# A four-layer graph network: the second layer's edge sum split between strips of a weighted matrix and gathers, with a small clear between all gathers

## The chip, the cores and the metric

The kernel runs on 1 core of one Trainium2 chip. The metric is the device time of one execution in microseconds (us), lower is better. Before the change the median of 3 runs is 6407.87 us (6407.16 to 6411.51).

## The reference, cut to what matters

A graph has 6250 nodes with 128 features and 100000 edges sorted by target; each layer's result is added to x and normalised. The four layers differ in how they sum over edges:

```python
edge_index = jnp.stack([src, dst])
x = _layernorm(x + _L0_gnn_ref(...))   # mean of h[dst] over src, twice; no weights
x = _layernorm(x + _L1_gnn_ref(...))   # the second layer:
    # msg = edge_weight[:, None] * x[src]
    # agg = segment_sum(msg, dst); h = relu((x + agg) @ W1 + b1); return h @ W2 + b2
x = _layernorm(x + _L2_gnn_ref(...))   # four propagation steps: segment_sum(x[src], dst) / degree, and attention
x = _layernorm(x + _L3_gnn_ref(...))   # h1 = relu([x[src], x[dst], edge_attr] @ W1.T + b1); sum over dst; a GRU cell
```

The targets are drawn as 6250 u^2, so the first edges crowd on few nodes: a tile of 128 sorted edges spans few targets at the start and many at the end.

## The kernel before, in words

The edges are cut into 784 tiles of 128; four tiles are a group, 196 groups. Everything is written out engine by engine, each engine works in its program order, and semaphores tie them; no planner decides anything. A stage ends with a barrier of all engines.

`prepare_edges` loads and transposes the edge lists and builds tables (indices, targets relative to a group's first target, unit offsets) with many short VectorE instructions on one partition. `build_adjacency` builds a dense 6272 x 6272 matrix of edge counts in bf16 in memory, strip by strip: for each tile it compares an iota with a key per edge (`hot`, line 656), multiplies it with a one-hot of the low source bits (line 725), and ScalarE copies the sums into a slab.

`dense_pass` multiplies that matrix with node rows split into three bf16 terms (21 matmuls for each of its blocks of 7 x 128 rows and 512 columns, line 1145). It is used twice in the first layer (all of the matrix, 91 blocks) and in each of the four steps of the third layer, where only a part of the matrix is multiplied and the remaining tiles are gathered beside it (line 1069): 244 tiles in steps 1 and 4, 344 tiles in steps 2 and 3.

`layer1_pass` is the second layer's edge sum, all by gathers. For each group POOL issues four indirect DMAs (line 1415, 128 rows of 512 bytes each), ScalarE scales the rows by the edge weights (line 1432), VectorE makes one-hots (line 1456), TensorE multiplies rows by one-hots, and a matrix of ones by one-hots for the degrees (lines 1492, 1493), and VectorE adds both results to the accumulator (line 1451). `layer1_nodes` then writes the degrees out and applies the layer's two matrices.

`message_pass` is the fourth layer's edge stage: 784 gathers (line 2139), and for each group edge features are loaded, transposed and multiplied, added to the gathered rows (`meet`, line 2206), rectified and summed.

Each of these passes is followed by a second version for graphs whose targets spread too widely, which is branched over here.

Of the kernel before, what the change touches and what calls it, by code (L numbers as in the profile page):

```python
# [59 lines left out]
AC = N + max(COLUMNS) + 6  # L60
FILLED = 320
# [30 lines left out]
def gnn_resnorm(nc, out, x, src, dst, edge_attr_128, edge_weight,  # L92
# [6 lines left out]
    with ctx:  # L99
# [84 lines left out]
        tail_loc = sb("tail_loc", [P, TAILS])  # L184
        tail_base = sb("tail_base", [1, TAILS // K + GU], I32)
# [15 lines left out]
        rdeg_row, deg_row, dinv_row = dram("rdeg_row", [NP]), dram("deg_row", [NP]), dram("dinv_row", [NP])  # L201
        loc_rows = dram("loc_rows", [TILES, P], I16)
# [117 lines left out]
        def prepare_edges():  # L320

            with ExitStack() as st:
# [16 lines left out]
                offs, bad = tmp("offs", [1, UP]), tmp("bad", [1, 6, UP])  # L339
# [3 lines left out]
                of_tile = tmp("of_tile", [1, 2, TILES])  # L343
                units = len(UNITS)
                with stage("cleared", "e_in", "dve_done", "turned", "copied", "info_out", "rows_out", "group_in", "info_in", "based",
                           "row_done", "spread", "col_done", "tabs_out") as (
                        block, cleared, e_in, dve_done, turned, copied, info_out, rows_out, group_in, info_in, based,
                        row_done, spread, col_done, tabs_out):
# [7 lines left out]
                    def _(sp):  # L356
# [24 lines left out]
                        sp.dma_start(dst_index, dst_idx[:, :]).then_inc(tabs_out, 16)  # L381
                        sp.wait_ge(rows_out, 32)
                        sp.wait_ge(tabs_out, 64)

                    @block.vector
                    def _(dve):
# [76 lines left out]
                        for heads, split in SPLITS.items():  # L463
# [16 lines left out]
                        after(40)  # L480
# [3 lines left out]
                        after(43)  # L484
                        nc.vector.tensor_scalar(offs[:, :], offs[:, :], 0.0, None, ALU.max).then_inc(row_done, 1)
                        nc.vector.tensor_reduce(worst[:, 0:1], worst[:, :], AX.X, ALU.max).then_inc(row_done, 1)
                        after(45)
# [16 lines left out]
                        nc.vector.tensor_tensor(two(again[:, :]), two(dst_c[:, :]), ps[:, 4:6, 0:TILES // 2], ALU.is_equal).then_inc(col_done, 1)  # L504
                        done(8)
                        for c in CLASSES:
# [26 lines left out]
                    def _(pe):  # L533
# [9 lines left out]
                        for n in range(2):  # L543
# [3 lines left out]
                            lastmm.then_inc(spread, 1)  # L547

# [392 lines left out]
        def dense_pass(n, table, heads, transposed=False, split=None, phases=()):  # L941
# [7 lines left out]
            with ExitStack() as st:  # L949
# [4 lines left out]
                adj = tmp("adj", [P, RING, GW, BLOCK], BF16)  # L954
                if groups:
                    rows = tmp("rows", [P, GR * K, heads * P])
                    onehot = tmp("onehot", [P, OH, K, P])
# [6 lines left out]
                with stage(*names) as (block, *s):  # L964
# [156 lines left out]
                    def _(pe):  # L1121
                        for t in range(tiles + 1):
# [11 lines left out]
                            if t == tiles:  # L1134
                                break
# [1348 lines left out]
```

## Time and profile before

| | us |
|---|---|
| median of 3 runs | 6407.87 |
| the profiled execution | 6403.48 |
| its span | 6401.9 |
| PE, DVE, ACT, POOL busy | 4821.9, 2547.6, 1447.4, 2736.0 |
| granted TensorE clock, mean | 0.882 |

Where the span goes, by the first and last instructions of the stages: the edge tables 0 to 112 us, the adjacency matrix to about 1000, the first layer to about 1970, the second layer's edge sum to 2967, the third layer from there to about 5240, the message pass from 5248 to about 6236, and the rest. Times below are microseconds from the start of the span. A row of the timeline gives the start, the length, the engine, the line, the tiles, how many instructions were merged, and in brackets how long the engine had been idle and who released it. fp32 matmuls stand in the records as two.

### The profile page before, as it was taken

To read this page: it belongs to the slowest core of one execution; us is meant where nothing else is said; L and a number is where in the kernel's file an instruction comes from. 1 tells how busy PE (TensorE), PEld (TensorE's weight loads), DVE (VectorE), ACT (ScalarE), POOL (GpSimd) and SP (SyncE) were. 2 spreads that over 40 slices of the span, in tenths; PEclk is the share of its full clock that TensorE was granted. 3 is DMA by queue.
4 is the path that set the end of the run, shared out by engine and by line. 5 is a ranking of instruction groups with operands and counts; after the bars stand their busy time and mean duration, and the time that the engine had idled before them with its cause. 6 is when DMAs were issued, how large, how long until landed. Compare 5 with 4: busy or idle time off the path is not lost. (4 is left out here: it accounts for less than half of the span.)

```text
span 6401.9 us, 87750 instructions
## 1 busy us (share of the span) xinstructions
PE 4821.9 (75%) x28467; PEld 3336.5 (52%) x28706; DVE 2547.6 (40%) x6483; ACT 1447.4 (23%) x2559; POOL 2736.0 (43%) x2767
## 2 busy tenths in 40 slices
PE   1677665997995556555798799989978967777675
PEld 0444333444444555554654376657656556676663
DVE  5678773001004222224546633252242354444445
ACT  0467772001002222222101100010010022222222
POOL 2000000000004777773355177557717727777770
PEclk6789887998997777777799899999999989989987
DMA  1166998997982222221565688688868755555541
GB/s 59 45 87 119 134 149 171 204 202 170 202 177 65 52 52 52 52 52 47 159 197 169 217 264 257 214 275 253 250 211 259 238 146 144 144 141 145 142 119 41
DMA packets 1485756, 973.04 MB, mean 152 GB/s; under 512 B 698166, under 2 KB 1407150, under 8 KB 1485424
## 3 DMA queue, kind: packets, MB, share of 16 engines
q1 hardware_dynamic: 1147613, 599.81, 38.3%
q0 software_dynamic: 99376, 228.31, 13.2%
q10 hardware_dynamic: 238500, 141.37, 7.7%
q8 instruction: 167, 2.74, 0.2%
q14 instruction: 100, 0.82, 0.0%
HBM read 652.10 MB, written 162.95 MB: 127 GB/s over the span
## 5 line engine op out<-in xcount | busy, mean ns | idle before, releaser
L1145 PE MATMUL ps<-adj_d,xs_d 128*128 128x512 bf16 (+1 forms) x7699 | 1704.8, 379 | 162.3 <-DVE xs_d L1114 149.2
L1145 PEld LDWEIGHTS ps<-adj_d,xs_d 128*128 128x128 bf16 x7938 | 782.5, 100 | 1023.4 <-DVE xs_d L1114 153.0
L1415 POOL DMA_INDIRECT rows_g<-x_tab,idx_g x784 | 743.0, 948 | 1246.0 <-ACT idx_g L1424 1007.4
L1069 POOL DMA_INDIRECT rows_d<-xh_tab,src_idx x688 | 697.6, 1014 | 446.9 <-POOLq L158 222.6
L2139 POOL DMA_INDIRECT rows_m<-p_tab,idx_m x784 | 750.9, 958 | 282.1 <-issue 237.8
L725 PE MATMUL ps<-hot,lo 128*128 128x500 bf16 (+4 forms) x2052 | 536.7, 385 | 299.7 <-DVE hot L656 153.2
L1492 PE MATMUL ps<-onehot_g,rows_g 128*128 128x128 f32 x1568 | 422.8, 363 | 426.1 <-ACT rows_g L1432 303.2
L1069 POOL DMA_INDIRECT rows_d<-x_tab,src_idx x488 | 489.5, 1003 | 537.7 <-POOLq L158 285.0
L767 ACT CAST slab<-ps 128x1000 f32 (+4 forms) x530 | 558.1, 1053 | 366.3 <-PE ps L743 167.2
L1492 PEld LDWEIGHTS ps<-onehot_g,rows_g 128*128 128x128 f32 x1568 | 333.5, 263 | 462.7 <-issue 303.8
L2266 PE MATMUL ps<-win_m,turned_hot_m 128*128 128x128 f32 x1568 | 330.5, 294 | 195.9 <-DVE pre_m L2206 195.1
L656 DVE TENSOR_SCALAR hot<-iota_key,key_col 128x1225 bf16<-128x1225 int16 (+4 forms) x782 | 414.9, 562 | 115.3 <-PE ps L743 73.7
L1131 PEld LDWEIGHTS ps<-onehot_d,rows_d 128*128 128x128 f32 x3728 | 443.2, 192 | 32.9 <-issue 16.9
L1131 PE MATMUL ps<-onehot_d,rows_d 128*128 128x128 f32 x3728 | 452.8, 276 | 2.0 <-DMA rows_d<-xh_tab,src_idx 2.0
L1432 ACT ACTIVATE rows_g<-rows_g,ew_col 128x128 f32<-128x128 f32 x784 | 271.8, 394 | 698.3 <-DMA rows_g<-x_tab,idx_g 698.3
L1044 ACT COPY acc<-ps 128x512 f32<-128x512 f32 (+1 forms) x54 | 31.0, 574 | 1706.2 <-PE ps L1145 1491.8
L1493 PE MATMUL ps<-onehot_g,ones_mat 128*128 128x128 f32 x1568 | 403.6, 350 | 0.0
L725 PEld LDWEIGHTS ps<-hot,lo 128*128 128x128 bf16 x2052 | 159.7, 103 | 444.2 <-ACT slab L767 204.8
L2266 PEld LDWEIGHTS ps<-win_m,turned_hot_m 128*128 128x128 f32 x1568 | 252.8, 203 | 225.1 <-issue 220.4
L1451 DVE TENSOR_TENSOR acc<-acc,ps 128x256 f32 x196 | 82.7, 422 | 676.9 <-PE ps L1493 676.9
L605 POOL MEMSET slab<- 128x6528 bf16 x1 | 5.5, 5537 | 808.3 <-DMA adjacency<-slab 808.3
L1493 PEld LDWEIGHTS ps<-onehot_g,ones_mat 128*128 128x128 f32 x1568 | 337.1, 265 | 0.0
(322 smaller groups left out, 6115.7 us busy)
## 6 DMA issues: line engine op xcount, KB each, us to landing
adj_d<-adjacency SPq DMA_DIRECT2D x196, 896.0 KB
attr_m<-in_edge_attr SPq DMA_DIRECT2D x195, 256.0 KB
k_rows_d<-k_tab ACTq DMA_DIRECT2D x56, 448.0 KB, 4.3
loc_m<-loc_rows SPq DMA_DIRECT2D x196, 128.0 KB
adjacency<-slab SPq DMA_DIRECT2D x4, 4900.0 KB
q_s<-q_tab SPq DMA_DIRECT2D x42, 448.0 KB
rden_s<-rden_tab SPq DMA_DIRECT2D x42, 448.0 KB
xh_tab<-rows_s ACTq DMA_DIRECT2D x42, 448.0 KB
```

The lines of the kernel that those rows point to most:

```text
L656: nc.vector.tensor_scalar(hot[:, t % HOT, 0:w], iota_key[:, 0:w], key_col[:, t:t + 1], None, ALU.is_equal).then_inc(hot_made, 1)
L725: last = nc.tensor.matmul(ps[:, bank(k, b), 0:to], lo1[:, slot, n, :], hot[:, t % HOT, b * w:b * w + to], start=(t == u.tile), stop=(k == ...
L767: nc.scalar.copy(slab(c)[:, 0:banks * u.per_bank, bass.ds(at[k % 8], u.width)].rearrange("p (b h) r -> p b h r", b=banks), ps[:, s:s + ban ...
L1069: nc.gpsimd.indirect_dma_start(rows[:, q % GR * K + k, :], None, table, bass.IndirectOffsetOnAxis(ap=src_idx[:, j:j + 1], axis=0)).then_in ...
L1131: last = nc.tensor.matmul(sums_of(q)[:, h, :], rows[:, q % GR * K + k, h * P:(h + 1) * P], onehot[:, q % OH, k, :], start=(k == 0), stop=( ...
L1145: last = nc.tensor.matmul(ps[:, m % 2, 0:w], xs[:, g * GW + k, e, :], adj[:, slot, k, 0:w], start=(g == 0 and k == 0 and e == 0), stop=(g ...
L1415: nc.gpsimd.indirect_dma_start(rows[:, j, :], None, x_tab, bass.IndirectOffsetOnAxis(ap=idx[:, q, k:k + 1], axis=0)).then_inc(rows_in[j // ...
L1432: last = nc.scalar.activation(rows[:, j, :], rows[:, j, :], ACT.Copy, scale=ew_col[:, bass.ds(i * U + j, 1)])
L1492: nc.tensor.matmul(sums_of(q)[:, 0, :], rows[:, j, :], hot, start=(k == 0), stop=(k == K - 1))
L1493: last = nc.tensor.matmul(sums_of(q)[:, 1, :], ones_mat[:, :], hot, start=(k == 0), stop=(k == K - 1))
L2139: nc.gpsimd.indirect_dma_start(rows[:, q, k, :], None, p_tab, bass.IndirectOffsetOnAxis(ap=idx[:, q, k:k + 1], axis=0)).then_inc(rows_in[2 ...
L2266: nc.tensor.matmul(ps[:, 2 + q % 2, c], turned_hot[:, q % 2, c], win[:, q % R, :], start=True, stop=False)
```

## The change

There are four parts.

1. `layer1_pass` is written anew. The first 292 tiles are no longer gathered. For each of them VectorE makes a one-hot of the source's low 7 bits (`lo1`, 128 columns) and one of a key made of the source's high bits and the target's place in a narrow window (`hot`, 343 or 490 columns); ScalarE multiplies `lo1` by three bf16 terms of the edge weight (`lo_w`); TensorE multiplies the three with `hot` into a strip; VectorE adds the strip into a `slab` of 49 x 144 columns in fp32. 98 tiles work in pairs of two to a unit, with 7 target columns (343 wide); 42 in pairs and 152 alone, with 10 (490 wide): 222 units. The units fall into 8 chunks. Behind each chunk a sweep reads all of x in 7 windows of 448 KB and multiplies them with the slab (49 fp32 matmuls of 144 columns), and ScalarE clears the slab. The other 492 tiles, 123 groups, are gathered as before, one group due about every 2.4 strip tiles. The matmuls with ones are gone; the accumulator holds one part instead of two.
2. The degrees now come from the first dense pass (`count=True`): VectorE sums each block of the matrix along its columns, and the sums are turned and written out at that stage's end.
3. `prepare_edges` makes the keys, the low bits and the strips' offsets, and writes them to memory.
4. In all three kinds of gathering passes POOL clears a 128 x 64 fp32 tile `pause` behind every gather (492 + 1176 + 784 = 2452 in all), and waits for the clear before the last one.

The branched-over version of the second layer's pass is now `general_pass` with weights.

```diff
@@ dense_pass (POOL)
                                     nc.gpsimd.indirect_dma_start(
                                         rows[:, q % GR * K + k, :], None, table,
                                         bass.IndirectOffsetOnAxis(ap=src_idx[:, j:j + 1], axis=0)).then_inc(rows_in[q % GR], 16)
+                                    if j > tail:
+                                        pool.wait_ge(paced, j - tail)
+                                    nc.gpsimd.memset(pause[:, :], 0.0).then_inc(paced, 1)
@@ dense_pass (VectorE, with count)
+                            if count and t < tiles:
+                                w = place(m // blocks, m % blocks)[2]
+                                dve.wait_ge(adj_in[t % RING], 16 * (t // RING + 1))
+                                nc.vector.tensor_reduce(parts[:, g * GW:(g + 1) * GW, m:m + 1], adj[:, t % RING, :, 0:w], AX.X, ALU.add).then_inc(tallied, 1)
@@ message_pass (POOL)
+                                    pool.wait_ge(paced, n * U + q * K + k + 1)
+                                    nc.gpsimd.sem_inc(begun, 1)
+                                    nc.gpsimd.memset(pause[:, :], 0.0).then_inc(paced, 1)
@@ layer1_pass (new)
+            GR, OH, AHEAD, BANKS, HOTS, XS = 10, 6, 4, 2, 3, 2
+                    for q in range(groups):
+                        due[q * WT // groups].append(q)
...
+                    @block.gpsimd
+                        for q in range(groups):
+                            if q >= GR:
+                                pool.wait_ge(group_done, q - GR + 1)
+                            for k in range(K):
+                                j = (first_group + q) * K + k
+                                nc.gpsimd.indirect_dma_start(
+                                    rows[:, q % GR, k, :], None, x_tab,
+                                    bass.IndirectOffsetOnAxis(ap=src_idx[:, j:j + 1], axis=0)).then_inc(rows_in[q % GR], 16)
+                                if q or k:
+                                    pool.wait_ge(paced, q * K + k)
+                                nc.gpsimd.memset(pause[:, :], 0.0).then_inc(paced, 1)
...
+                    @block.scalar
+                        def blanken(c):
+                            if c:
+                                act.wait_ge(x_used, c * G)
+                            nc.scalar.copy(slab[:, :, :], zero[:, 0:1].unsqueeze(2).to_broadcast([P, WIN, WC])).then_inc(blank, 1)
...
+                        def weigh(t):
+                            act.wait_ge(lo_made, t + 1)
+                            if t >= HOTS:
+                                act.wait_ge(stripped, WUNIT_OF[t - HOTS] + 1)
+                            for e in range(TERMS):
+                                last = nc.scalar.activation(lo_w[:, t % HOTS, e, :], lo1[:, t % HOTS, :], ACT.Copy, scale=weight[:, e, t:t + 1])
+                            last.then_inc(lo_weighted, 1)
...
+                        for t in range(WT):
+                            weigh(t)
+                            for q in due[t]:
+                                scale(q)
+                            if t in sweep_at:
+                                blanken(sweep_at[t] + 1)
...
+                    @block.vector
+                        for t in range(WT):
+                            pick(t)
+                            u = WUNIT_OF[t]
+                            if t == WUNITS[u].tile and u >= 2:
+                                enter(u - 2)
+                            for q in due[t]:
+                                match(q + AHEAD)
+                                add(q)
...
+                    @block.tensor
+                        for t in range(WT):
...
+                            for e in range(TERMS):
+                                last = nc.tensor.matmul(strip(u), lo_w[:, t % HOTS, e, :], hot[:, t % HOTS, 0:w],
...
+                            for q in due[t]:
+                                sum_group(q)
+                            if t in sweep_at:
+                                sweep(sweep_at[t])
```

`add(q)` waits for `group_done` of group q; `sum_group(q)` waits for the scaled rows, the one-hots and the add two groups back; `pick` makes `lo1` and `hot`; `enter` adds a strip to the slab.

On POOL, at the head of the message pass, before (the four gathers of a group follow one another):

```order
240 L2139 DMA rows_m<-p_tab,idx_m 128x128 x4
241 L2136 REGISTER_ALU
242 L2139 DMA rows_m<-p_tab,idx_m 128x128 x4
243 L2136 REGISTER_ALU
244 L2139 DMA rows_m<-p_tab,idx_m 128x128 x4
```

and now:

```order
3551 L2356 DMA rows_m<-p_tab,idx_m 128x128
3552 L2359 ISA
3553 L2361 MEMSET pause 128x64
3554 L2356 DMA rows_m<-p_tab,idx_m 128x128
3555 L2359 REGISTER_ALU
3556 L2361 MEMSET pause 128x64
```

Between any two gathers there now stands a clear, and a semaphore step ahead of it.

On DVE in the second layer's pass, before (L1456 makes a group's one-hots; the add, L1451, comes behind the one-hots of the groups ahead):

```order
1463 L1456 TENSOR_SCALAR onehot_g<-iota,loc_col 128x128
1464 L1456 ISA
1465 L1456 TENSOR_SCALAR onehot_g<-iota,loc_col 128x128
1466 L1456 ISA
1467 L1456 TENSOR_SCALAR onehot_g<-iota,loc_col 128x128
1468 L1456 ISA
1469 L1456 TENSOR_SCALAR onehot_g<-iota,loc_col 128x128
```

and now, in the later part where each tile is a unit of its own (L1644 and L1645 are `pick`, L1657 `enter`, L1616 `match`, L1631 `add`):

```order
2081 L1657 TENSOR_TENSOR slab_g<-slab_g,ps 128x49x10
2082 L1616 TENSOR_SCALAR onehot_g<-iota,loc_col 128x128 x4
2083 L1631 ISA
2084 L1631 TENSOR_TENSOR acc<-acc,ps 128x128
2085 L1644 TENSOR_SCALAR lo_g<-iota,lo_g 128x128
2086 L1645 TENSOR_SCALAR hot_g<-iota_key_g,key_g 128x490
2087 L1644 TENSOR_SCALAR lo_g<-iota,lo_g 128x128
2088 L1645 TENSOR_SCALAR hot_g<-iota_key_g,key_g 128x490
```

The one-hot `lo1` of the next strip tile stands behind the add of the group before it.

On PE in the same pass, before (rows and ones in turn):

```order
3022 L1492 MATMUL ps<-onehot_g,rows_g 128x128
3023 L1493 MATMUL ps<-onehot_g,ones_mat 128x128
3024 L1492 MATMUL ps<-onehot_g,rows_g 128x128
3025 L1493 MATMUL ps<-onehot_g,ones_mat 128x128
3026 L1492 MATMUL ps<-onehot_g,rows_g 128x128
```

and now, around the first sweep (L1707 are strips, L1683 a gathered group, L1694 the sweep):

```order
3105 L1707 MATMUL ps<-hot_g,lo_w_g 128x490 x6
3106 L1683 MATMUL ps<-onehot_g,rows_g 128x128 x4
3107 L1707 MATMUL ps<-hot_g,lo_w_g 128x490 x6
3108 L1694 MATMUL ps<-slab_g,xp_g 128x144 x49
3109 L1707 MATMUL ps<-hot_g,lo_w_g 128x490 x3
3110 L1683 MATMUL ps<-onehot_g,rows_g 128x128 x4
```

Strips, groups and sweeps share one in-order queue.

## Rows read from the trace of the kernel before

**Rows 1.** The page, part 5: the message pass's gathers (busy, mean ns, idle before):
```profile
L2139 POOL DMA_INDIRECT rows_m<-p_tab,idx_m x784 | 750.9, 958 | 282.1 <-issue 237.8
```

**Rows 2.** Busy times in stretches (length; PE, PEld, DVE, ACT, POOL; clock; DMA):
```profile
1120.00:1280.00 160.00, 159.21 (x728) 72.50 (x741) 0.00 (x0) 2.93 (x5) 0.00 (x0) 1.00 0.95 204
2500.00:2600.00 100.00, 57.92 (x320) 54.05 (x320) 25.59 (x104) 29.11 (x100) 75.62 (x81) 0.78 0.21 52
3800.00:3850.00 50.00, 49.74 (x325) 35.38 (x329) 12.63 (x53) 0.59 (x1) 36.78 (x39) 1.00 0.82 249
5600.00:5650.00 50.00, 39.02 (x288) 37.13 (x288) 22.51 (x75) 12.84 (x32) 37.81 (x41) 0.87 0.54 143
```

**Rows 3.** Timeline of the second layer's edge sum, its gathers, and its start:
```profile
1976.11 0.48 ACT L1424 COPY idx_g<-src_idx 128x4 int32<-128x4 int32 x4 [0.77 <-PEq L158]
...
2299.07 0.94 POOL L1415 DMA_INDIRECT rows_g<-x_tab,idx_g  x1 [0.30 <-issue]
2300.32 0.94 POOL L1415 DMA_INDIRECT rows_g<-x_tab,idx_g  x1 [0.30 <-ACT idx_g L1435]
```

**Rows 4.** The adds of that pass, line L1451 (min/median/max ns, first and last start):
```profile
L1451 DVE TENSOR_TENSOR acc<-acc,ps x196: 420/422/424, 1996.0 to 2966.9; 128x256 f32 x196
```

**Rows 5.** Who waited for whom (total us, times, longest): 3640 to 4180, then 5300 to 6200:
```profile
POOL rows_d L1069 <- issue: 102.1, 335, 0.3
POOL rows_d L1069 <- PE ps L1131: 9.7, 8, 2.1
...
DVE pre_m L2206 <- DMA rows_m<-p_tab,idx_m: 379.8, 134, 5.0
```

**Rows 6.** Timeline of the second layer's edge sum, one group at two TensorE clocks:
```profile
2302.41 0.63 PE L1493 MATMUL ps<-onehot_g,ones_mat 128*128 128x128 f32 x2
2302.83 0.64 PE L1492 MATMUL ps<-onehot_g,rows_g 128*128 128x128 f32 x2
...
2309.80 0.39 ACT L1432 ACTIVATE rows_g<-rows_g,ew_col 128x128 f32<-128x128 f32 x1
2310.33 0.46 PE L1492 MATMUL ps<-onehot_g,rows_g 128*128 128x128 f32 x2 [2.72 <-ACT rows_g L1432]
2311.84 0.69 ACT L1432 ACTIVATE rows_g<-rows_g,ew_col 128x128 f32<-128x128 f32 x2 [1.57 <-DMA rows_g<-x_tab,idx_g]
2311.97 0.39 PE L1493 MATMUL ps<-onehot_g,ones_mat 128*128 128x128 f32 x2
2312.58 0.42 DVE L1451 TENSOR_TENSOR acc<-acc,ps 128x256 f32 x1 [3.54 <-PE ps L1493]
2312.92 1.03 DVE L1456 TENSOR_SCALAR onehot_g<-iota,loc_col 128x128 f32<-128x128 int16 x4
```

**Rows 7.** Timelines elsewhere: short and wide instructions of DVE and ACT:
```profile
74.86 0.28 DVE L413 COPY ends<-infos 1x278 f32<-1x278 f32 x1
175.49 0.61 DVE L656 TENSOR_SCALAR hot<-iota_key,key_col 128x490 bf16<-128x490 int16 x2 [0.79 <-PE ps L736]
1978.93 10.72 DVE L1444 MEMSET acc<- 128x12800 f32 x1 [7.94 <-issue]
3050.75 0.94 ACT L1617 COPY xg_k<-xT 128x896 f32 x1 [6.23 <-PE ps L1596]
3054.71 2.02 DVE L1639 TENSOR_REDUCE knorm_k<-kk_k 128x14 f32<-128x1792 f32 x1
```

**Rows 8.** The page, part 6: one 448 KB load, us to landing:
```profile
k_rows_d<-k_tab ACTq DMA_DIRECT2D x56, 448.0 KB, 4.3
```

**Rows 9.** POOL's timeline: memsets after one another, and a gather after a wait:
```profile
0.91 0.20 POOL L280 MEMSET ident<- 128x128 f32 x1 [0.29 <-POOLq L2474]
1.06 0.20 POOL L281 MEMSET ones_mat<- 128x128 f32 x1
...
3210.16 2.03 PE L1131 MATMUL ps<-onehot_d,rows_d 128*128 128x128 f32 x16
3211.57 0.94 POOL L1069 DMA_INDIRECT rows_d<-x_tab,src_idx  x1 [1.86 <-PE ps L1131]
```

More of the change, by code:

```diff
@@ L60 @@
 AC = N + max(COLUMNS) + 6
+WT, WPAIRS, WNARROW = 292, 70, 49
+WUnit = namedtuple("WUnit", "tile tiles width")
+WUNITS = [WUnit(2 * k, 2, 7 if k < WNARROW else 10) for k in range(WPAIRS)]
+WUNITS += [WUnit(t, 1, 10) for t in range(2 * WPAIRS, WT)]
+WUNIT_OF = [k for k, u in enumerate(WUNITS) for n in range(u.tiles)]
+WFIRSTS = (0, 49, 74, 102, 128, 152, 176, 199)
+WENDS = WFIRSTS[1:] + (len(WUNITS),)
+WC = 144
+WKEYS = WIN * 10
+WROW = 224
 FILLED = 320
@@ L966, in dense_pass @@
                     at = RING + SPLIT + GR
-                    high, left, middle, low, used, stored, cleared, matched, group_done, added = s[at:at + 10]
-                    at += 10
+                    high, left, middle, low, used, stored, cleared, matched, group_done, added, tallied, deg_turned, deg_copied, deg_out, paced = s[at:at + 15]
+                    at += 15
                     for work in works:
@@ new lines, in layer1_pass @@
+                part, left = tmp("part", [P, WT], BF16), tmp("left", [P, WT])
+                at = tmp("at", [1, WROW + len(WFIRSTS)], I32)
+                zero = tmp("zero", [P, 1])
+                names = [f"rows_in{q}" for q in range(GR)] + [f"x_in{k}" for k in range(XS)]
+                names += ["tabs_in", "listed", "cleared", "terms", "matched", "scaled", "group_done", "added", "hot_made", "lo_made",
+                          "lo_weighted", "stripped", "entered", "blank", "x_used", "paced"]
@@ L1480, in _ @@
+                        for u in range(len(WUNITS) - 2, len(WUNITS)):
+                            enter(u)
+                        place(len(WFIRSTS) - 1, len(after_group) + len(after_place))
                     @block.tensor
                     def _(pe):
[L1482 to L1494 removed]
@@ L1496, in _, with sum_group @@
-                        rounds(nc.tensor, f"wide_g{tag}_pe", wide_path, steps, step)
+                        def sum_group(q):
+                            pe.wait_ge(matched, q + 1)
+                            if q >= BANKS:
+                                pe.wait_ge(added, after_group[q - BANKS])
+                            pe.wait_ge(scaled, q + 1)
+                            for k in range(K):
+                                last = nc.tensor.matmul(sums_of(q), rows[:, q % GR, k, :], onehot[:, q % OH, k, :], start=(k == 0), stop=(k == K - 1))
+                            last.then_inc(group_done, 1)
@@ new lines, in sweep @@
+                        def sweep(c):
+                            pe.wait_ge(entered, WENDS[c])
+                            if c:
+                                pe.wait_ge(added, after_place[c - 1])
+                            for g in range(G):
+                                n = c * G + g
+                                pe.wait_ge(x_in[n % XS], 16 * (n // XS + 1))
+                                for k in range(GW):
+                                    last = nc.tensor.matmul(ps[:, 6, 0:WC], xp[:, n % XS, k, :], slab[:, g * GW + k, :],
+                                                            start=(g == 0 and k == 0), stop=(g == G - 1 and k == GW - 1))
+                                last.then_inc(x_used, 1)
```

334 lines of the change are left out of this document (229 added, 105 removed).

## The prediction

> **What bounds the kernel now.** I read the page first, then busy times by stretch, then the timelines inside the two stages whose POOL rows look alike, then the waits. In the second layer's edge sum POOL issues a gather every 1.25 us (start to start in [rows 3]; 81 in 100 us in [rows 2]). Each takes 0.94 us and is followed by 0.30 us in which POOL waits for nothing that the profile shows, while PE is busy 58 us of 100, DVE 26, ACT 29 [rows 2]. So POOL sets the pace: 784 x 1.25 = 980 us, and the pass runs from 1976.1 [rows 3] to the add at 2966.9 and its 0.42 us [rows 4], 991 us. The message pass is the same picture: 784 gathers of 0.958 us, mean, with 238 us of bare issue between them [rows 1], and `meet` waits 380 us for gathered rows [rows 5]. Its pitch is 50 us / 40.2 = 1.245 us (busy 37.81 of 50 in [rows 2], with gap 0.30). In the third layer's steps 2 and 3 two engines are at their limit: PE is busy 49.74 of 50 us at full clock [rows 2], and POOL, with 335 of some 344 gathers behind a bare 0.3 us in step 2, waits for PE 9.7 us in all [rows 5]. In the first layer's dense passes PE is busy 159.21 of 160 us [rows 2].
>
> **The second layer's pass.** POOL falls from 784 to 492 gathers: 492 x 1.25 = 615 us if the pitch stays. That would save 365 us, if the other engines kept up, and by busy time they seem to: ACT has 3 x 292 + 492 = 1368 activations at 0.30 us (a pair ends in 0.69, one in 0.39 [rows 6]) and 8 slab clears, some 450 us; DVE comes to about 460 (292 x 0.52 for `lo1` and `hot`, 492 x 0.26, 222 x 0.65, 123 x 0.29, by the durations below). But the order of the instructions ties them into one chain. At a tile on which a group is due, DVE makes `lo1`; ACT weighs it three times, then scales four gathered tiles; PE can only then do the group; DVE waits for the group to add it, and only behind this add stands the next tile's `lo1`. The chain, from rows:
> - DVE `lo1` until ACT can start: 0.35 us (a compare of 128 columns lasts 0.30 where four take 1.03 [rows 6]).
> - ACT: seven activations, six pitches of 0.30, and 0.53 from the last one's start to PE's (2309.80 to 2310.33 [rows 6]): 2.33.
> - PE: an fp32 matmul of 128 x 128 takes 0.23 at the high clock (2310.33 to 2311.97 is seven of them) and 0.42 at the low (2302.41 to 2302.83) [rows 6]. I take 0.30, since the granted clock was 0.78 [rows 2] and PE will again be half idle: four are 1.20.
> - PE to DVE: the last of the eight matmuls starts at 2311.97 and takes 0.23, the add starts at 2312.58 [rows 6]: 0.39. The add, half as wide as that one of 0.42, 0.29.
> Sum 4.56 us for each of 123 such tiles, 561 us. The other 169 tiles are paced by DVE: `lo1` 0.25, `hot` 0.27 (two of 490 columns in 0.61, [rows 7], where one lasts 0.34), `enter` of 490 fp32 columns at about 1.1 us per 1000 (896-column rate of the sum of 1792 in 2.02 [rows 7]) with its start, 0.7: 1.22 us, 206 us.
> A sweep is 49 fp32 matmuls of 144 columns, 49 x 0.30 x 144/128 = 16.5 us, but needs seven loads of 448 KB with two in flight; one lands in 4.3 us [rows 8], so I take 20. Behind it ACT clears 7056 columns before it may weigh: at 0.94 us for 896 less a start of 0.3 [rows 7] some 5.3 us. PE stands still for that. Seven sweeps at 25.3 and the last at 20: 197 us. The start is the clear of `acc` (half of 10.72 [rows 7]) and the first slab clear, 11 us.
> Together 561 + 206 + 197 + 11 = 975 us against 991: 16 us less. Almost all of POOL's gain is lost, and POOL has 360 us to spare at its present pitch. Bounds: with the high clock throughout and loads hidden, 123 x 0.28 + 8 x 4 less, 910; with the low clock throughout, 123 x 0.48 and 8 x 3 more (49 x 0.42 x 144/128 is 23 us a sweep), 1058.
>
> **The edge tables.** Some 36 short instructions on one partition at about 0.28 us (278 columns [rows 7]), a few wider, and three more stores ahead of the barrier: 11 us more (6 to 16).
>
> **The degrees.** 3584 bf16 columns for each block at 1.13 ns (2.02 us for 1792 [rows 7]) are 4.0 us on DVE, idle there [rows 2]; PE needs 21 x 0.219 = 4.6 us for a block (159.21 / 728 [rows 2]). So they are hidden, but for the first seven, narrow ones (1.0 us each, beside the split of the rows) and the turn and store at the end: 6 us (3 to 12). The matmuls with ones and the accumulator's second half that go were on no path but the old pass's.
>
> **The clears.** Nothing in this trace stands between two gathers, so the price must be bounded. From above: a clear of 64 columns costs by itself at most the pitch of two clears of 128 columns, 0.91 to 1.06, 0.15 us [rows 9]; halved by its columns, 0.09. Added whole to each gather the pitch is 1.34 to 1.40. From below: the gap of 0.30 goes and the clear takes its place, 0.94 + 0.09 = 1.03. For the lower end speaks this: the gap is no preparation that every gather needs. The one at 3211.57 had waited for PE, where the first of two groups (half of the 2.03 us from 3210.16 [rows 9]) ended at 3211.18, 0.39 us before: no more than DVE needs behind PE in [rows 6]. The gap appears behind a gather, at the turn to the next; and POOL starts an ordinary clear 0.05 us before the record of the last one ends [rows 9]. If a clear can start so in the gather's tail, and a gather so behind a clear, the pitch is 0.94 + 0.15 = 1.09. I take 1.09, nearest to the row of the two clears, and keep 1.03 and 1.40 as the ends.
> In the message pass that is 784 x (1.245 - 1.09) = 122 us less. What is late next is PE: 39.0 of 50 us [rows 2] is 3.9 us a group, and four gathers would take 4.36. In the second layer it changes nothing, by the chain above. In the third layer PE is full, so a faster POOL gives nothing.
> The Trainium skill speaks against me here (Perfetto Trace Analysis, DMA Instruction — SWDGE (GPSIMD)): the recorded end is the writing of the last descriptor, and the core goes on to complete the instruction after it. By that rule the 0.30 us is the gather's own work, no clear can use it, and the sum would be that of the first rival; the gather after a wait, told above, fits either. No row here has another instruction behind a gather.
>
> **The sum.** 6403.5 - 16 + 11 + 6 - 122 = 6282.5 us for the profiled execution; the median of the runs is 4.4 us above that execution, so 6287.
>
> **The rivals.**
> *The clear is added whole* (slower). At 1.335 us the message pass, which has no slack on POOL, costs 784 x 0.09 = 71 us more. Steps 2 and 3 of the third layer have 16 gathers of lead, and behind that POOL becomes the bound: 2 x 344 x 0.09 = 62, and step 4 244 x 0.09 = 22; I count half, 42. With the other terms: 6403.5 + 1 + 71 + 42 + 4.4 = 6522. It decides from any pitch above 1.25, since the rest of the change comes to +1. At 1.40 it is near 6640. For it: no row shows the gap filled. Against it: the gap is the same 0.30 whatever the load.
> *The clear hides in the gap.* Pitch 1.245 as before: 6403.5 + 1 + 4.4 = 6409, no change. For it: 0.09 fits into 0.30.
> *The strips run by busy time, not by the chain.* Then the pass takes POOL's 615 us or less, plus the last sweep and start, 31: 646, which is 345 less. With the clears as forecast (POOL 536, the others some 560): 5960; without, 6080. For it: three engines near 450 us of work. Against it: the rows of the order, in which the add stands before the next `lo1`.
>
> **How the numbers follow.** The forecast has 0.48, the whole clear 0.29, the hidden clear 0.14, the free strips 0.07, and 0.02 for none of these. The forecast's own range is 6200 to 6370 (pitch 1.03 to 1.15 and a layer of 910 to 1058, not both at an end). The range for 8 in 10 reaches from there to the whole clear at 0.09: 6170 to 6535; left out are the free strips and a clear of 0.15. A measurement tells 0.2%, 13 us. The second layer's error of tens of us splits the hidden clear in 0.05, 0.05 and 0.04. Faster: 0.47 of the forecast + 0.05 + 0.07 = 0.59. Same: 0.01 + 0.05 + 0.01 of the rest = 0.07. Slower: 0.29 + 0.04 + 0.01 = 0.34.
>
> **What would show it.** In the second layer's pass: length 975 us, PE waiting for `lo_w` for some 380 us, DVE for the group's matmuls, POOL for PE for hundreds. The sweeps: 20 us each, PE waiting for x windows. In the message pass: gathers 1.09 us apart, and `meet` still waiting for them. In the first dense pass: length unchanged. I am wrong if a gather still starts 0.30 us behind the last one with the clear's time on top, or if strips follow each other in under 2.1 us a tile.

## Result, and the profile after

| kernel | median of its runs, us | range, us |
|---|---|---|
| before | 6407.51 (4 runs) | 6404.36 to 6411.51 |
| changed | 6461.68 (4 runs) | 6454.14 to 6467.5 |

The ratio is 1.0081, 95% interval 1.0069 to 1.0093: the change makes the kernel 54 us slower. I had forecast 6287 us and a faster kernel; the time is inside the range, the sign is wrong. The profiled execution spans 6452.5 us where before spanned 6401.9, which is 50.6 us more.

POOL's gathers are the first thing to read. The groups of POOL's instructions in the changed kernel (busy, mean ns, idle before, releasers) have the message pass (L2356, against [rows 1]), the second layer's (L1545) and steps 2 and 3 of the third layer (L1136):

```profile
L2356 POOL DMA_INDIRECT rows_m<-p_tab,idx_m x784 | 752.0, 959 | 173.6 <-POOL pause L2361 112.4 <-ACT idx_m L2520 44.4 <-issue 13.5
L1545 POOL DMA_INDIRECT rows_g<-x_tab,src_idx x492 | 478.6, 973 | 310.0 <-PE ps L1683 247.2 <-issue 50.3
L1136 POOL DMA_INDIRECT rows_d<-xh_tab,src_idx x688 | 707.1, 1028 | 328.2 <-POOLq L168 219.2 <-issue 99.2 <-PE ps L1208 1.6
```

The idle time before the message gathers fell from 282 to 174 us, but 784 clears now stand there as well. POOL's timeline in the middle of that pass (start, duration, engine, line, in brackets the idle time before) shows how one turn is made up:

```profile
5399.91 0.95 POOL L2356 DMA_INDIRECT rows_m<-p_tab,idx_m  x1 [0.16 <-POOL pause L2361]
5400.87 0.17 POOL L2361 MEMSET pause<- 128x64 f32 x1
5401.19 0.95 POOL L2356 DMA_INDIRECT rows_m<-p_tab,idx_m  x1 [0.16 <-POOL pause L2361]
5402.15 0.17 POOL L2361 MEMSET pause<- 128x64 f32 x1
5402.47 0.95 POOL L2356 DMA_INDIRECT rows_m<-p_tab,idx_m  x1 [0.16 <-POOL pause L2361]
```

The clear does start at once at the gather's recorded end, as forecast, and takes 0.17 us. The next gather, however, does not follow at once: 0.16 us of the old gap of 0.30 [rows 3] stay. 0.95 + 0.17 + 0.16 is a pitch of 1.28 us. The pass's first and last gathers start at 5263.0 and 6284.3 us, 1021.3 us apart; before it was 988.6. Those are 32.7 of the 50.6 us.

The same four stretches as in [rows 2], after:

```profile
1120.00:1280.00 160.00, 159.21 (x728) 72.57 (x742) 136.83 (x36) 2.93 (x5) 0.00 (x0) 1.00 0.93 202
2500.00:2600.00 100.00, 65.44 (x271) 42.29 (x270) 40.79 (x137) 45.77 (x128) 52.02 (x92) 0.72 0.23 63
3800.00:3850.00 50.00, 49.74 (x325) 35.34 (x328) 12.51 (x52) 0.59 (x1) 43.76 (x79) 1.00 0.81 244
5600.00:5650.00 50.00, 36.30 (x270) 34.71 (x269) 19.61 (x63) 11.21 (x27) 42.99 (x75) 0.86 0.53 135
```

In the first row DVE is now busy 136.8 of 160 us with the degrees and PE as full as before: they are hidden. In the second no engine is busy two thirds of the time. The last row's 270 matmuls against 288 say little by themselves: in the kernel before alone, stretches of 50 us in this pass hold from 237 to 320. Over the whole pass PE's records are the same 5480, in 1021 us where before it was 988.

Who waited for whom in the second layer's edge sum of the changed kernel (1984 to 2975 us; total us, times, longest):

```profile
DVE acc L1631 <- PE ps L1683: 354.2, 123, 4.0
ACT lo_w_g L1571 <- DVE lo_g L1644: 323.7, 155, 3.3
...
POOL rows_g L1545 <- PE ps L1683: 247.2, 66, 31.3
...
PE ps L1707 <- DVE hot_g L1645: 159.3, 93, 2.4
ACT slab_g L1557 <- PE ps L1694: 157.5, 7, 26.1
```

DVE stands before 123 adds, one for each group, for 2.9 us apiece; ACT waits for DVE's `lo1`; POOL has to wait for PE. The timeline shows the ring once around, with a group and two tiles in it:

```profile
2601.70 0.29 DVE L1631 TENSOR_TENSOR acc<-acc,ps 128x128 f32 x1 [2.95 <-PE ps L1683]
...
2601.91 0.25 DVE L1644 TENSOR_SCALAR lo_g<-iota,lo_g 128x128 bf16<-128x128 int16 x1
...
2602.19 2.04 ACT L1571 ACTIVATE lo_w_g<-lo_g,weight_g 128x128 bf16<-128x128 bf16 x6 [2.81 <-DVE lo_g L1644]
...
2604.13 1.26 ACT L1563 ACTIVATE rows_g<-rows_g,ew_col 128x128 f32<-128x128 f32 x4
...
2605.54 2.04 PE L1683 MATMUL ps<-onehot_g,rows_g 128*128 128x128 f32 x8 [0.43 <-ACT rows_g L1563]
...
2607.72 0.29 DVE L1631 TENSOR_TENSOR acc<-acc,ps 128x128 f32 x1 [2.89 <-PE ps L1683]
```

From add to add it is 6.02 us; by my terms 4.56 for the group's tile and 1.22 for the other are 5.78. And the end of a sweep, where PE's last columns, ACT's clear and the next weighing follow each other:

```profile
2625.99 1.98 PE L1694 MATMUL ps<-slab_g,xp_g 128*128 128x144 f32 x14 [1.78 <-DMA xp_g<-x_tab]
2628.01 6.07 ACT L1557 COPY slab_g<-zero_g 128x7056 f32<-128x7056 f32 x1 [22.61 <-PE ps L1694]
2633.99 0.98 ACT L1571 ACTIVATE lo_w_g<-lo_g,weight_g 128x128 bf16<-128x128 bf16 x3
```

From the sweep's first matmul at 2607.38 to the clear's end it is 26.7 us (forecast 25.3).

### The profile page after: what moved, and what is told of

It reads as the page before. It is cut to its first block and busy times, and to the rows that moved or that the text cites. A ratio compares the mean times of both kernels' runs of the same rounds, so it can differ in the third digit from the quotient of the medians.

```text
span 6452.5 us, 89590 instructions
## 1 busy us (share of the span) xinstructions
PE 4885.3 (76%) x27978; PEld 3210.3 (50%) x28217; DVE 3032.0 (47%) x7067; ACT 1631.9 (25%) x2948; POOL 2913.6 (45%) x4928
## 3 DMA queue, kind: packets, MB, share of 16 engines
q14 instruction: 153, 1.25, 0.1%
## 5 line engine op out<-in xcount | busy, mean ns | idle before, releaser
L1136 POOL DMA_INDIRECT rows_d<-xh_tab,src_idx x688 | 707.1, 1028 | 328.2 <-POOLq L168 219.2
L2356 POOL DMA_INDIRECT rows_m<-p_tab,idx_m x784 | 752.0, 959 | 173.6 <-POOL pause L2361 112.4
L1136 POOL DMA_INDIRECT rows_d<-x_tab,src_idx x488 | 490.5, 1005 | 555.4 <-POOLq L168 384.3
L1545 POOL DMA_INDIRECT rows_g<-x_tab,src_idx x492 | 478.6, 973 | 310.0 <-PE ps L1683 247.2
L1707 PE MATMUL ps<-hot_g,lo_w_g 128*128 128x490 bf16 (+1 forms) x876 | 290.0, 473 | 303.2 <-DVE hot_g L1645 159.3
L1172 DVE TENSOR_TENSOR acc<-acc,ps 128x256 f32 (+1 forms) x294 | 107.0, 364 | 563.4 <-PE ps L1208 552.4
L2427 DVE TENSOR_TENSOR pre_m<-ps,rows_m 128x512 f32<-128x512 f32 x196 | 135.3, 690 | 494.8 <-DMA rows_m<-p_tab,idx_m 453.8
L1571 ACT ACTIVATE lo_w_g<-lo_g,weight_g 128x128 bf16<-128x128 bf16 x876 | 281.3, 390 | 327.2 <-DVE lo_g L1644 323.7
L1192 DVE TENSOR_REDUCE parts_d<-adj_d 128x7 f32<-128x3584 bf16 (+1 forms) x91 | 332.3, 3670 | 54.6 <-DMA adj_d<-adjacency 54.4
```

Of the source, the lines that this page charges most:

```text
L1136: nc.gpsimd.indirect_dma_start(rows[:, q % GR * K + k, :], None, table, bass.IndirectOffsetOnAxis(ap=src_idx[:, j:j + 1], axis=0)).then_in ...
L1192: nc.vector.tensor_reduce(parts[:, g * GW:(g + 1) * GW, m:m + 1], adj[:, t % RING, :, 0:w], AX.X, ALU.add).then_inc(tallied, 1)
L1545: nc.gpsimd.indirect_dma_start(rows[:, q % GR, k, :], None, x_tab, bass.IndirectOffsetOnAxis(ap=src_idx[:, j:j + 1], axis=0)).then_inc(row ...
L1571: last = nc.scalar.activation(lo_w[:, t % HOTS, e, :], lo1[:, t % HOTS, :], ACT.Copy, scale=weight[:, e, t:t + 1])
L1707: last = nc.tensor.matmul(strip(u), lo_w[:, t % HOTS, e, :], hot[:, t % HOTS, 0:w], start=(t == unit.tile and e == 0), stop=(t == unit.til ...
L2356: nc.gpsimd.indirect_dma_start(rows[:, q, k, :], None, p_tab, bass.IndirectOffsetOnAxis(ap=idx[:, q, k:k + 1], axis=0)).then_inc(rows_in[2 ...
```

## The experiments

The first four ran beside the kernel before at 6407.67 us (13 runs), as in the result.

**The change without its clears.** Edit, in all three places:

```
-    pool.wait_ge(paced, n * U + q * K + k + 1)
-    nc.gpsimd.sem_inc(begun, 1)
-    nc.gpsimd.memset(pause[:, :], 0.0).then_inc(paced, 1)
```

> The changed kernel without any of the 2452 clears. Theory 1 (the clears are the whole loss: they fill the gap of 0.30 us behind a gather and push the next gather 0.035 to 0.04 us later, which costs where POOL sets the pace): gathers 1.25 us apart again, the message pass about 33 us shorter, the third layer about 10 us shorter, the second layer's edge sum unchanged at 988 us; 6415 us in all, the old time within 10. Theory 2 (the loss of the message pass comes from elsewhere in the change, the clears being free): 6460, unchanged. Theory 3 (a clear helps the gathers of the second layer's pass): that pass gets longer than 988 us.

Measured: 6414.06 us (10 runs), ratio 1.0010 (1.0000 to 1.0019). The clears cost the changed kernel 47.6 us, and all else in the change together costs 6 (0 to 12 by the interval). The turn is the old one again, and the message pass is back at 988.5 us (5261.5 to 6250.0):

```profile
L2350 POOL DMA_INDIRECT rows_m<-p_tab,idx_m x784 | 750.8, 958 | 281.3 <-issue 237.4 <-ACT idx_m L2510 42.7 <-ACT idx_m L2528 1.2
```

In the third layer the gathers of `xh_tab` span 1016.1 us where with the clears they span 1027.9.

**The kernel before with the clears alone.** The same three lines put behind each gather of its three passes.

> The kernel before, with a clear and its wait behind every gather of all three kinds of pass (784 + 1176 + 784), nothing else changed. Theory 1: the old second-layer pass, paced by POOL, also pays 784 x 0.035 to 0.04 = 30 us, so that with the message pass (33) and the third layer (10) the time is 6407 + 73 = 6480. Rival (the clears cost only in the message pass, where a semaphore step also stands between gather and clear): 6450, and if its loop of the second layer, written the same way, pays too, 6480 with the third layer unchanged.

Measured: 6493.97 us, ratio 1.0141 (1.0124 to 1.0158), 86 us more where 73 were expected. By stage: second layer +38, message pass +33, gathers of `xh_tab` +13.5. Its second layer, which POOL paced, pays; that of the changed kernel, which the ring paces, does not. So the price belongs to the clear, not to the strips, and it is paid where POOL is the bound: 784 x (1.28 - 1.245) is 27, and the measured 33 to 38 are a little more. In the message pass of the changed kernel the clears take 0.184 us in the mean (144.0 us for 784), so that 0.959 + 0.184 + 0.16 stands against 0.958 + 0.30, which is 35 us.

**Clears of 256 columns.** `pause = sb("pause", [P, 256])`.

> The changed kernel with clears of 256 columns instead of 64. A clear of 128 columns took 0.15 us start to start, so one of 256 is about 0.25 to 0.28, still under 0.30. Theory 1 (the clear runs inside the gap that stands behind a gather anyway): pitch stays near 1.29 us, message pass within 10 us, 6462 to 6475 in all. Rival (the gap shrank from 0.30 to about 0.15 and the clear is added to it): pitch 1.28 + 0.16 = 1.44 us, message pass 125 us longer, third layer up to 90 longer, some 6620 to 6680; the second layer's edge sum unchanged in either case, since POOL is not its bound.

Measured: 6741.4 us, ratio 1.0521 (1.0503 to 1.0539), above the rival's 6620 to 6680 as well: the message pass is 147 us longer than in the changed kernel, the gathers of `xh_tab` 101, and the stretch from the second layer's first gather to the third's 26, where none was expected. POOL in the message pass:

```profile
5501.55 0.33 POOL L2361 MEMSET pause<- 128x256 f32 x1
5502.04 1.00 POOL L2356 DMA_INDIRECT rows_m<-p_tab,idx_m  x1 [0.17 <-POOL pause L2361]
5503.02 0.34 POOL L2361 MEMSET pause<- 128x256 f32 x1
5503.53 0.95 POOL L2356 DMA_INDIRECT rows_m<-p_tab,idx_m  x1 [0.16 <-POOL pause L2361]
```

The remainder behind the clear is the same 0.16 (0.17 once); what the clear is longer is added whole. So a fixed 0.14 of the gap goes, and the clear costs 0.17 for 64 columns and 0.33 for 256.

**The add one group later.** Nothing is left out: a group's sum is added when the next one falls due, and the last behind the loop.

```
                             for q in due[t]:
                                 match(q + AHEAD)
-                                add(q)
+                                if q:
+                                    add(q - 1)
...
+                        add(groups - 1)
```

> The changed kernel, where VectorE adds each gathered group one group later (behind the one-hots of the next due group), so that the next strip tile's lo1 no longer waits for the group just begun. Nothing is left out. Theory 1 (the order of the instructions ties DVE, ACT and PE into one chain of about 4.5 us for each tile with a group): the second layer's edge sum falls from 988 us to between 740 and 800, paced then by POOL, whose 492 gathers at 1.29 us need 635, and the sweeps; 6210 to 6280 in all. Rival (the sweeps and the work itself set the length, and the wait for the add only covers other waits): 950 to 988 us, 6430 to 6460 in all.

Measured: 6223.6 us, ratio 0.9716 (0.9699 to 0.9732), with the clears still in. From the start of the pass to the third layer's first gather it is 905 us (1987.9 to 2893.1) against 1145 (1984.8 to 3129.7): 240 us are regained by the place of one instruction. The busy times over the pass, of the changed kernel and then of this one:

```profile
1985.00:2973.00 988.00, 614.79 (x2644) 385.70 (x2644) 399.89 (x1436) 472.78 (x1376) 567.17 (x985) 0.72 0.22 60
```

```profile
1987.00:2735.00 748.00, 495.76 (x2630) 327.74 (x2630) 394.38 (x1436) 463.10 (x1377) 569.26 (x985) 0.86 0.30 79
```

DVE, ACT and POOL did the same work. PE's matmuls, as many, took 119 us less: the granted clock was 0.86 where it was 0.72, with PE busy 0.66 of the stretch where it was 0.62. DVE's wait for the group before the add fell from 354 us to 56, and POOL's for PE from 247 to 39. What stands in the list now:

```profile
ACT slab_g L1559 <- PE ps L1698: 161.6, 7, 24.4
...
PE ps L1687 <- ACT rows_g L1565: 106.4, 107, 3.8
...
ACT rows_g L1565 <- DMA rows_g<-x_tab,src_idx: 70.7, 39, 3.3
...
DVE acc L1633 <- PE ps L1687: 55.7, 39, 3.8
```

**Fourteen more runs, on four other chips.** There the kernel before itself took 7184 to 7229 us, 12 to 13% more, so whole times are compared only with the runs of before on the same chip. "The first chip" is that of the runs above. Each of the four was used on one occasion only, so what is put down to the chip here could also be the occasion. The kernels are the pair again; the change without clears; with clears of one column (`[P, 1]`); with the late add and no clears; and that with four buffers for the windows of x:

```
-GR, OH, AHEAD, BANKS, HOTS, XS = 10, 6, 4, 2, 3, 2
+GR, OH, AHEAD, BANKS, HOTS, XS = 10, 6, 4, 2, 3, 4
```

| kernel | ratio to before on the same chip (95%) |
|---|---|
| before, again | 1.0003 (0.9989 to 1.0017) |
| changed | 0.9844 (0.9826 to 0.9862) |
| changed, no clears | 0.9818 (0.9775 to 0.9860) |
| changed, clears of 1 column | 0.9852, 0.9832, 0.9827 (each within 0.003) |
| late add, no clears | 0.9715, 0.9716, 0.9710 (each within 0.003) |
| late add, no clears, four windows | 0.9638, 0.9619, 0.9630, 0.9635 (each within 0.003) |
| late add, clears of 64, four windows | 0.9641 (0.9621 to 0.9661) |

Expected of the clears of one column, in three runs:

> The changed kernel with `pause` one column wide instead of 64: as many clears, waits and increments, hardly any data. Theory A (the gap of 0.30 us behind a gather shrinks to 0.16 behind a clear, whatever the clear's length, and the clear's own time is added; the clears of 64 and 256 columns, 0.17 and 0.33 us, give 0.83 ns a column, so one of 1 column takes 0.12): pitch 0.95 + 0.12 + 0.16 = 1.23 us against 1.245 without a clear, message pass 964 us or so against 988.5, but other stages hardly move; whole time 6390 to 6414 us, where the kernel without clears took 6414.1. Rival B (any instruction between two gathers, with its wait and increment, costs a fixed 0.17 us, and the width counts only beyond 64 columns): pitch 1.28, time 6455 to 6462, as in the changed kernel. Rival C (the gap goes wholly when the clear writes next to nothing): pitch below 1.10, time below 6320.

> The clears one column wide, again, since on the chip of the last runs the kernel before took 12% longer and engines stood in bare issue in every stage, so the whole times of those runs can't be set beside the earlier ones. In their undisturbed stretches the gather took 0.94, the one-column clear 0.12 and the rest 0.19, a pitch of 1.25. Theory A' (what remains behind a clear is 0.16 to 0.19, the clear's own time comes on top): message pass within 5 us of 988.5 and a whole time within 10 us of the kernel without clears. Rival B (a fixed price for any instruction between): 6455 to 6462 on a chip where the kernel before takes 6407.

> On a chip like the first: pitch 0.94 + 0.12 + 0.19 = 1.25, message pass 985 to 995 us, whole time 6410 to 6425, like the kernel without clears (6414). Rival: 6455 to 6462, a fixed price for any clear. On a chip like the second: 0.983 to 0.985 of the kernel before, which tells nothing on it.

The turn can be read in stretches that nothing disturbs (the message pass, second of these runs):

```profile
6102.38 0.12 POOL L2361 MEMSET pause<- 128x1 f32 x1
6102.69 0.95 POOL L2356 DMA_INDIRECT rows_m<-p_tab,idx_m  x1 [0.19 <-POOL pause L2361]
6103.64 0.11 POOL L2361 MEMSET pause<- 128x1 f32 x1
6103.94 0.95 POOL L2356 DMA_INDIRECT rows_m<-p_tab,idx_m  x1 [0.19 <-issue]
```

0.95 + 0.12 + 0.19 is 1.25 or so: the smallest clear just fills what its presence saves. A fixed price of 0.17, or a gap that goes wholly, are both out. The whole times can't decide here, since the changed kernel with and without its clears can't be told apart on these chips either, and the small clears were not measured on a chip like the first.

Expected of the change without clears, as it is, and of before:

> The changed kernel without clears once more, as the measure beside it on the same chip: 1.001 times the kernel before, as measured earlier, if the chip is one like the first; on a chip like the second it tells how much of that chip's loss falls on the strips.

> The changed kernel as it is. On a chip like the second (kernel before about 7200 us): if the clears cost there what they cost on the first chip, 0.982 + 0.0075 = 0.990; rival, if they hide because POOL no longer paces the message pass (its one-column clears cost 13 us there, within the spread), 0.983. On a chip like the first: 1.008 again.

> The kernel before, for its profile on this chip. On a chip like the second, theory: its second layer's edge sum, with 784 gathers and more than twice the matmuls of the groups, loses about as much as the message pass there (a third), 991 to 1100 or more us, where the changed kernel's pass lost 51; rival: all stages lose alike and the difference lies in the first layer. Ratio 1.000.

The surprise is the sign: there the change, clears and all, gives 110 us (7075.7 against 7186.0, on the one of these chips where it ran as it is). From the second layer's first gather to the third layer's first, the kernel before takes 1336 us there (1981.2 to 3317.5) against 1149 on the first chip, +187; the changed one 1198 (1989.1 to 3187.4) against 1144, +54. What comes ahead of these passes is not slower: the first gather of before stands at 1981.2 where it stood at 1977.3, against the rival that put the loss into the first layer. Of the 786 us that before loses, 187 lie there, 254 in the third layer and 330 in the message pass, which takes 1319 and 1315 us in the two kernels. POOL waits 344 and 287 us in it for ACT's copies of the indices, where on the first chip it hardly waited behind its start, so POOL no longer paces it and its clears have cover. What POOL still does at its old pitch (0.30 us gaps), the others can't use. The kernel before, second layer, POOL, ACT and DVE:

```profile
2506.53 0.95 POOL L1415 DMA_INDIRECT rows_g<-x_tab,idx_g  x1 [0.31 <-issue]
2510.43 0.19 ACT L1435 COPY idx_g<-src_idx 128x4 int32 x1 [12.69 <-DMA h_tab<-h_rows]
2510.45 0.42 DVE L1451 TENSOR_TENSOR acc<-acc,ps 128x256 f32 x1 [13.67 <-DMA h_tab<-h_rows]
```

and PE in the message pass of the change without clears:

```profile
5906.05 0.59 PE L2477 MATMUL ps<-win_m,turned_hot_m 128*128 128x128 f32 x2 [1.33 <-issue]
...
5908.18 0.59 PE L2477 MATMUL ps<-win_m,turned_hot_m 128*128 128x128 f32 x2 [1.11 <-issue]
...
5910.31 0.37 PE L2478 MATMUL ps<-wts,attr_T_m 128*128 128x128 f32 x1 [1.33 <-issue]
```

PE pauses over a microsecond between matmuls for nothing that the profile shows, and DVE and ACT wait some 13 us. On the first chip the same kernel had 3.7 us of such idle time before all its matmuls of L2477, where here it has 198.5, and none at all before those of L2478, where here it has 74.3 (group of the page, first chip: busy, mean ns, idle):

```profile
L2478 PE MATMUL ps<-wts,attr_T_m 128*128 128x128 f32 x1568 | 319.7, 287 | 0.0
```

The kernel before shows the same in the second layer. On the first chip none of PE's idle time before L1492 is bare issue; here it is most of it (total us, times, longest):

```profile
PE ps L1492 <- issue: 412.5, 73, 18.6
```

The transfer named as releaser of DVE and ACT, `h_tab<-h_rows`, was issued before 255 us and writes a table that this pass doesn't read, so I take that name as wrong; what DVE and ACT need next is PE's group, and PE stands. The gathers' packets took no longer: by part 3 of the two pages 13.2% of 6402 us is 845 us of the 16 engines, and 11.7% of 7188 is 841. Why PE stands is not found. In the second layer PE's bare issue comes to 412 us in the kernel before and to 105 us before the strips (L1707) in the changed one, so before meets more of it there.

Expected of the late add without clears, three times, and with four windows, four times, once more with the clears:

> The late add of before (a group's sum is added when the next group falls due) and no clears at all. If the two effects are independent, the time is 6223.6 less the 47.6 us that the clears cost the changed kernel: 6176 us. Theory A: the second layer's pass is then paced in part by POOL (in the run with the late add POOL's rows show 110 us of idle time for 492 gathers, half of it bare issue), so the missing clears may give a few more: 6165 to 6180. Rival: in that pass the clears were hidden in POOL's waits for PE and give nothing, 6180 to 6190.

> Late add and no clears. On a chip where the kernel before takes 6407: 6165 to 6180 if the two effects add (theory), 6180 to 6190 if the clears were hidden in the second layer.

> Late add, no clears. On a chip like the first 6165 to 6190 us; on one like the second 0.972 times the kernel before, as twice.

> The same with four buffers for the windows of x (XS = 4) instead of two, so that four of a sweep's seven loads of 448 KB can be in flight or landed when the sweep starts. Theory: the eight sweeps are paced by their loads (a sweep from its first matmul to the slab's clear lasts 20.6 us where 49 matmuls of 315 ns take 15.4), so up to 5 us each go: 6165 to 6180 less 25 to 40, 6130 to 6150. Rival: PE's matmuls in a sweep are bound by the low clock and the order of the columns, and the loads are hidden; then no change from the run without the four buffers.

> The same with four window buffers: 25 to 40 us less than the run with two if the sweeps are paced by their loads. On the second chip it was 59 us less. Rival: loads hidden, no change.

> The same with four window buffers. On a chip like the first 25 to 40 us less than g3; on one like the second 0.963 times the kernel before, as twice.

> On a chip like the first: 6223.6 - 47.6 - 25 to 40 = 6136 to 6151 us. Rival: window loads are hidden, 6165 to 6180. On a chip like the second: 0.963 of the kernel before.

> As the last one but with the clears of 64 columns. It repeats the price of the clears with a faster second layer: 47 us more than the same without them if only the message pass and the third layer pay; up to 15 us more than that if the second layer's pass is by then paced by POOL; less, if a slower POOL eases the other engines' stalls.

Whether the two effects add on a chip like the first stays unmeasured. On the others the late add is worth less: 71 us or 1.0% on the one chip that ran the change without clears both ways (7093.0 and 7022.0 us), with 72 us of it in the second layer, where on the first chip it was worth 238 (with the clears in both). Four windows give another 55 to 61 us (25 to 40 expected). The sweeps' matmuls with two windows and with four (busy, mean ns, idle before them):

```profile
L1692 PE MATMUL ps<-slab_g,xp_g 128*128 128x144 f32 x784 | 128.1, 327 | 75.1 <-DMA xp_g<-x_tab 65.7 <-issue 5.2 <-DVE slab_g L1653 4.2
```

```profile
L1692 PE MATMUL ps<-slab_g,xp_g 128*128 128x144 f32 x784 | 114.3, 309 | 19.4 <-issue 14.5 <-DMA xp_g<-x_tab 3.9 <-DVE slab_g L1653 1.0
```

56 us of idle time go and 14 of work: the loads did pace the sweeps. The clears cost nothing that can be told there (6936.5 against 6926.1 us, intervals that overlap; 47 were expected). Late add, no clears and four windows is the best kernel on these chips; on the first, the late add alone (6223.6) beats both kernels by 2.8% and more.

## Why the prediction was wrong

Stage by stage, the change forecast and the change that the two profiled executions show:

| term | forecast, us | measured, us |
|---|---|---|
| second layer's pass | -16 | -3.4 (991.2 to 987.8) |
| edge tables | +11 | +10.1 |
| adjacency matrix, not changed | 0 | -3.6 (922.8 to 919.2) |
| first layer, with the degrees | +6 | +2.2 |
| message pass | -122 | +32.7 |
| third layer, gathers of `xh_tab` | 0 | +11 |
| the rest | 0 | +1.6 |
| sum | -121 | +50.6 |

**The step that failed is "the pitch is 0.94 + 0.15 = 1.09".** 155 of the 172 us of error are its 784 gathers. It had two halves. "A clear can start so in the gather's tail" held: 5399.91 + 0.95 is 5400.86, and the clear starts at 5400.87. "And a gather so behind a clear" failed: it starts 0.16 us behind it, for 64 columns and for 256. The price of the clear itself, 0.15 taken and 0.17 measured, was nearly right. What stands there now is a turn of 0.95 + 0.17 + 0.16, 1.28 us. My argument from the gather at 3211.57 [rows 9] showed only that a gather which has waited needs no long preparation behind the event; its 0.39 us between the last matmul's end and its start could hold 0.16 us of it, and I didn't count that. A turn whose fill had never been seen was priced from two ends without a middle: 0.16 us of it stayed with every clear. Whether these belong to the gather that comes, to the clear or to its semaphore stays open, since no run had a filler of another kind or one without its semaphore. One row speaks for the gather: in the changed kernel the first gather of the second layer follows an iota that ends at 1985.31, with no gather ahead of it.

```profile
1985.60 7.13 POOL L1545 DMA_INDIRECT rows_g<-x_tab,src_idx  x1 [0.29 <-issue]
```

The Trainium skill (Perfetto Trace Analysis, DMA Instruction — SWDGE (GPSIMD)) has the core work on behind the recorded end, and gives no length for it. Here the clear starts 0.01 us behind that end and 0.14 of the 0.30 us vanish, so for that half of the gap the trace does not bear it out as work that keeps the next instruction off; for the other 0.16 it is undecided on which side of the turn it lies.

**The rivals.** The whole clear (6522, from any pitch above 1.25) had the right side, and at 1.28 its condition was met. But it let the whole gap stay and halved the clear to 0.09, two errors that partly cancel: it priced the message pass at +71 us where +33 came. The truth lies between it and the clear that hides in the gap. Where it put 42 us into the third layer, 11 came, with POOL's waits for PE in steps 2 and 3 down to 1.6 us (17.1 without clears): there PE hardly keeps POOL waiting any more, and I read it as POOL having become the bound there as well. The forecast that a faster POOL gives nothing there said nothing of a slower one.

**The ring in the second layer was right**, and it was the larger of the two questions: 292 gathers, 365 us of POOL's time, were gone, and 3 us came back. The edit that moves one add shows it: 240 us. Its terms: a group and a tile 5.78 forecast, 6.02 in the turn shown; a sweep 25.3 and 26.7; the clock 0.78 taken from [rows 2], 0.72 granted. DVE's waits for the group come to 354 us, and POOL waited 247 us for PE, as forecast. PE's waits before the strips were fewer than the 380 us forecast: 81 us under the name of `lo_w` and 159 under that of `hot`. In the turn shown `hot` had been ready since 2602.47 and PE started at 2603.28, just behind ACT's third activation, so part of those 159 belong to `lo_w` too. The busy-time rival (6080) failed as long as the order stood; with the order changed the pass takes 748 us, not 646, so even then the loads of the sweeps and ACT's slab clears count.

**The tables** came within 1 us. **The degrees** are hidden: 91 reductions of 3.67 us mean in a pass in which DVE was idle. Of the 6 us for the ends some 2 came: the next stage's first activation starts 5.1 us behind the start of the dense pass's last copy, where before it was 3.3. The 3.6 us less in the matrix, which the change doesn't touch, are scatter: it took 919 to 924 us in the executions profiled on the first chip.

**The chances.** Of the 0.59 for faster 0.47 rested on the pitch alone, with a rest of the change at +1 (measured +6 without clears). That the time lies inside 6170 to 6535 is no merit of the pitch of 1.09: alone it reached to 6370, and the wider range took in the rival. The evidence for 1.09 was one gather behind a wait, and the bounds, 1.03 to 1.40, had 1.245 well inside; nothing in them preferred one side so clearly.

## What to carry to other kernels

A gap between two instructions can have a part that stays whatever stands in it: before you count on filling it, find a row where something stands in it, or price the filler in full. When work is taken off the engine that sets the pace, follow one turn of the order across the engines; if a result is consumed ahead of the work that feeds the next result, consume it one turn later. And the worth of a change can differ from chip to chip, even in sign: here the change was 1.008 on one and 0.984 on another, and the late add gave 238 us on the first and 71 on another, where PE paused and no cause was found.

## What the runs showed of the hardware

- Behind a gather a clear starts at once (0.01 us), and the next gather 0.16 us behind the clear for 64 and 256 columns, 0.19 behind one of 1 column, where without a clear the gap is 0.30. Clears of 1, 64 and 256 columns took 0.12, 0.17 and 0.33 us.
- The same fp32 and bf16 matmuls took 615 us at a granted clock of 0.72, in a stretch of 988 us, and 496 at 0.86, in one of 748.
- Four chips ran the kernel before 12 to 13% slower than the first. On the one where it was profiled the first 1980 us took no longer, and the loss lies in the stages with gathers (187, 254 and 330 of 786 us): gathers of the same 0.95 us, but 412 us in which PE stands before L1492 with no wait that the profile shows, up to 18.6 us at a time.
